# One tile of gathered rows in every 27 quads comes by single-row DMAs of SyncE in place of a GpSimd gather

## The chip, the core and the metric

The kernel runs on one core of a Trainium2 chip. The metric is the device time of one execution in microseconds (us); lower is better. The engines of the core work through instruction lists of their own and meet only at semaphores: TensorE (PE in the profile, PEld for its weight loads), VectorE (DVE), ScalarE (ACT), GpSimd (POOL) and SyncE (SP), which here does nothing but register work and DMA issues. A name with a q behind it (SPq, ACTq) is the instruction queue of an engine.

## What is computed

A graph layer over 12,500 nodes with 160 features each (64 scalars and 32 vectors of three components) and 400,000 edges, sorted by their target node. All is float32.

```python
h_s, h_v = s @ lin1_ws * a, v @ lin1_wv * a            # per node, scaled
w = silu(edge_scalars @ fc_w1) @ fc_w2                 # per edge: 224 weights
es, ev = h_s[edge_src], h_v[edge_src]                  # per edge: one row of the table h
m_s1 = w1 * es * e0;  m_s2 = w4 * einsum(ev, e1)
m_v1 = (w2 * es) * e1;  m_v2 = w3 * ev * e0;  m_v3 = w5 * cross(ev, e1)
agg = segment_sum([m_s1, m_s2, m_v1, m_v2, m_v3], edge_dst)
out = layernorm(x + gated(sc + agg @ lin2))            # per node
```

What matters here is `h[edge_src]`: for each edge a row of 160 floats (640 bytes) of the table `h_table` in DRAM, at an arbitrary place.

## The kernel before, in words

`setup_block` (the first 100 us) scales the weights, computes `h_table` and stores it in DRAM, and loads the edge indices into SBUF. `edge_block` then does all the rest. Its edges, padded, make 3128 tiles of 128 edges, one edge to a partition. Four tiles (`QT`) make a **quad**, 782 in all; eight quads (`RING`) make a **round**, of which there are 97 and a rest of six quads. For a quad q the engines do this, each in its own list:

- GpSimd: `gather` (line 637), one indirect DMA for each tile, which reads 128 rows of `h_table` by the 128 indices of that tile into `rows`, a ring of 8 quads of 4 tiles. Each adds to the semaphore `rows_loaded[q % 8]`. At every second quad the first gather also waits on `tiles_summed`, so that GpSimd is at most about three quads ahead of the sums. Its list is written out in full, all 3128 gathers.
- ScalarE: loads `es` (the edge scalars, once for two quads), the activation `hid`, the copy `tsum` of the tiles' sums, and `copy_out`, which copies the sum of a quad into `aggsb[q % 2]` and signals `agg_copied`. Before it overwrites `aggsb[b]` it waits for the store of two quads earlier (`agg_stored[b]`).
- TensorE, in this order in the list of a quad: `weights` of the next quad (`psw`), for even q `hidden` (`psx`), now and then a piece of node work, `combine` of the quad before (`psg`, lines 955 and 957), and `sum_tiles` of this quad (`pst_e`, line 947), which waits on `prod_ready`.
- VectorE: `products` multiplies the weights in `psw` with the gathered `rows` into `prod` (lines 523, 533, 534) and signals `prod_ready`. It waits on `w_ready` and on `rows_loaded`. Then come the `shifts` (line 804).
- SyncE, one **turn** for each quad (`quad`, lines 549 to 557): read the quad's base row from SBUF into a register (`value_load`, line 549), wait for `agg_copied`, wait until the store before has landed, and store the sum with one DMA of 4 x 32 pieces of 640 bytes whose address is in a register (line 557). In turn 1 of a round come four more DMAs (`node_load`, lines 565 to 568) that load what 128 finished nodes need, in turn 7 one (`node_store`, line 573).

Node work (transposes, `lin2`, gates, layer norm) for 128 nodes goes along with each round from the third on. SyncE, TensorE, ScalarE and VectorE run the rounds in loops (`Fori`), GpSimd does not. An `Else` branch for unusual inputs is not run here.

Of the kernel before, what the change touches and what calls it, by code (L numbers as in the profile page):

```python
# [12 lines left out]
ds = bass.ds  # L13
# [42 lines left out]
PICK = [(B3X, 1), (B2A, 1), (B5X, 2), (B5X, 1)]  # L56

CHUNKS = K4 * F // P

C_W = HID ** -0.5 * 16.0 ** -0.5  # L60
C_S = C_W * SO ** -0.5
# [351 lines left out]
def edge_block(nc, io, m):  # L413

    with ExitStack() as ctx:
        def sb(name, shape, dt=F32):
            return ctx.enter_context(nc.sbuf_tensor(name, shape, dt))

        def sem(name):
            return ctx.enter_context(nc.semaphore(name))  # L420
# [2 lines left out]
        hid = sb("hid", [P, 2 * CH])  # L423
        idx = sb("idx", [P, 1], I32)
        rows = sb("rows", [P, RING * QT, F])
        prod = sb("prod", [P, 2, QT, PW])
        hot = sb("hot", [P, 2, 2 * QT, W8])
        sel = sb("sel", [P, 2, QT, K4, W8])
# [37 lines left out]
        w_ready = sem("w_ready")  # L466
        loads_seen = sem("loads_seen")
        rows_loaded = [sem(f"rows_loaded{u}") for u in range(RING)]
        hot_ready = sem("hot_ready")
        prod_ready = sem("prod_ready")  # L470
        shifts_ready = sem("shifts_ready")
# [71 lines left out]
        @block.sync  # L543
        def _(sp):
            miss = sp.value_load(m.misses[0:1, 0:1], min_val=0, max_val=CHECKS * P)

            def quad(q, i, b, free):

                at = sp.value_load(m.base[0:1, ds(q, 1)], min_val=0, max_val=N - 1)
                sp.wait_ge(agg_copied, q + 1)  # L550
                sp.sem_inc(loads_seen, 1)
                if b:
                    sp.wait_ge(agg_stored[0], 16 * (i + 1))
                elif free:
                    sp.wait_ge(agg_stored[1], 16 * i)
                sp.sem_inc(loads_seen, 1)
                sp.dma_start(m.agg[ds(at, W), :].rearrange("n (k c) -> k n c", k=K4),
                             aggsb[:, b, :]).then_inc(agg_stored[b], 16)

            def node_load(k, width, bufs, c, free):  # L560
                if free:
                    sp.wait_ge(n_res, k)
                sp.sem_inc(loads_seen, 1)
                nodes, r = ds(k * P, width), slice(0, width)
                sp.dma_start(bufs[0][r, :], m.agg[nodes, :]).then_inc(n_in[c], 16)
                sp.dma_start(bufs[1][r, :], io["x"][nodes, :]).then_inc(n_in[c], 16)
                sp.dma_start(bufs[2][:, r], io["xT"][0:S, nodes]).then_inc(n_in[c], 16)
                sp.dma_start(bufs[3][:, r], io["xT"][S:F, nodes]).then_inc(n_in[c], 16)

            def node_store(k, width):  # L570
                sp.wait_ge(n_norm, k + 1)
                sp.sem_inc(loads_seen, 1)
                sp.dma_start(io["out"][ds(k * P, width), :], yn[0:width, :]).then_inc(n_out, 16)

            def round_of(R, quads, first, loading, storing):
                for u in range(quads):
                    quad(R * RING + u, R * (RING // 2) + u // 2, u % 2, not first or u >= 2)
                    if loading and u == 1:
                        node_load(R - 2, P, main_bufs, 0, storing)
                    if storing and u == RING - 1:  # L580
                        node_store(R - 3, P)

            with sp.If(miss == 0):
                round_of(0, RING, True, False, False)
                round_of(1, RING, False, False, False)
                round_of(2, RING, False, True, False)
                with sp.Fori(3, ROUNDS) as R:
                    round_of(R, RING, False, True, True)
                round_of(ROUNDS, REST, False, True, True)
                for b in range(2):  # L590
                    sp.wait_ge(agg_stored[b], 16 * (QUADS // 2))
                node_load(NBLK - 2, P, spare_bufs(0), 1, False)
                node_load(NBLK - 1, LASTN, spare_bufs(1), 2, False)
                for k in range(ROUNDS - 3, NBLK):
                    node_store(k, P if k < NBLK - 1 else LASTN)
                sp.wait_ge(n_out, 16 * NBLK)
            with sp.Else():
                sp.wait_ge(g_zero, 1)
                with sp.Fori(0, AGG_ROWS // P) as b:
                    sp.dma_start(m.agg[ds(b * P, P), :], gsum[:]).then_inc(g_cleared, 16)  # L600
                sp.wait_ge(g_cleared, 16 * (AGG_ROWS // P))

                def tile(q, u, first):
                    if not first:
                        sp.wait_ge(g_added, 16 * (QT * q + u))
                        sp.sem_inc(loads_seen, 1)
                    h = S * (u % 2)
                    sp.dma_start(es[0:S, 0:P], io["esP"][h:h + S, ds(q * CH + P * (u // 2), P)]).then_inc(g_es, 16)
                    sp.dma_start(dstrow[:], io["dst"][ds(QT * q + u, 1), :].to_broadcast([P, P])).then_inc(g_dst, 16)

                for u in range(QT):
                    tile(0, u, u == 0)
                with sp.Fori(1, QUADS) as q:
                    for u in range(QT):
                        tile(q, u, False)
                sp.wait_ge(g_added, 16 * TILES)
                node_load(0, P, main_bufs, 0, False)
                with sp.Fori(1, NBLK - 1) as k:
                    node_store(k - 1, P)
                    node_load(k, P, main_bufs, 0, True)  # L620
                node_store(NBLK - 2, P)
                node_load(NBLK - 1, LASTN, main_bufs, 0, True)
                node_store(NBLK - 1, LASTN)
                sp.wait_ge(n_out, 16 * NBLK)
# [3 lines left out]
        def _(pool):  # L628
# [12 lines left out]
            with pool.If(miss == 0):  # L641
                for q in range(QUADS):
                    for j in range(QT):
                        gather(q, j, max(0, q - 2) if j == 0 and q % GROUP == 0 and q >= GROUP else 0)
            with pool.Else():
                with pool.Fori(0, TILES) as t:
# [128 lines left out]
        def _(dve):  # L775
# [9 lines left out]
            def products(I, u, first):  # L785
# [10 lines left out]
                    sel[:, b, :, :, :], hot[:, u // 2 % 2, QT * b:QT * b + QT, :].unsqueeze(2).to_broadcast([P, QT, K4, W8]),  # L796
                    m.e4[:, ds(q * QT, QT), :].unsqueeze(3).to_broadcast([P, QT, K4, W8]), ALU.mult)
                dve.wait_ge(w_ready, q + 1)
                dve.wait_ge(rows_loaded[u], 16 * QT * (I + 1))
                vec = rows[:, QT * u:QT * u + QT, :]  # L800
                all_products(prod[:, b, :, :], psw[b], vec, QT).then_inc(prod_ready, 1)
                if not first:
# [66 lines left out]
            with dve.If(miss == 0):  # L869
                nc.vector.memset(prod[:, :, :, V * 7:V * 8], 0.0)  # L870
                round_of(0, RING, True, False, False)
                with dve.Fori(1, 3) as I:
                    round_of(I, RING, False, False, False)
                round_of(3, RING, False, True, False)
                with dve.Fori(4, E4_ROUNDS) as I:
                    round_of(I, RING, False, True, True)
                dve.wait_ge(e4_loaded, 16 * E4_PIECES)
                with dve.Fori(E4_ROUNDS, ROUNDS) as I:
                    round_of(I, RING, False, True, True)
                round_of(ROUNDS, REST, False, True, True)  # L880
                node_normalise(ROUNDS - 3, P, True)
# [236 lines left out]
```

## Time and profile before

| | us |
|---|---|
| median of 3 runs | 4938.19 |
| lowest and highest run | 4926.22, 4938.32 |
| span of the profiled execution, first to last instruction | 4099.4 |
| TensorE busy in it | 4024.1 (98%) |
| GpSimd busy in it | 2993.0 (73%) |
| VectorE busy in it | 2439.2 (60%) |
| ScalarE busy in it | 2021.4 (49%) |

The profiled execution has no time of its own on record; beside its span of 4099.4 us stands the median of the runs, 838.8 us longer. This part lies before the first and behind the last instruction, and no row shows it. The granted TensorE clock is 0.995 of full speed over the span. Busy time of TensorE is modelled: consecutive matmuls overlap in the record, so that 98% does not mean that it never waited. SyncE's register work and DMA issues are not counted as busy, and its idle time stands only in the view of who waits for whom.

### The profile page before, as it was taken

The page shows a single profiled execution, that of the slowest core. Times are in us where ns is not written, and L with a number is a line of the kernel's source. Part 1 is how long each engine was busy: PE and PEld are TensorE (multiplying, and loading weights), DVE is VectorE, ACT ScalarE, POOL GpSimd, SP SyncE. Part 2 cuts the span into 40 slices and gives each one's busy share as a digit, 9 for nine tenths or more (in the row PEclk, how much of TensorE's full clock was granted, in tenths as well). Part 3 has the DMA queues.
Part 4 walks back from the last instruction along what each step waited for, and adds up shares of the span by engine and source line. Part 5 has one row for each costly group of instructions (what it writes and reads, how often), then busy time and mean ns, then how long its engine had stood idle before and what let it go on. Part 6 is the DMA issues. An engine that isn't in the chain of part 4 may idle for free.

```text
span 4099.4 us, 69550 instructions
## 1 busy us (share of the span) xinstructions
PE 4024.1 (98%) x15455; PEld 1725.2 (42%) x15455; DVE 2439.2 (60%) x7618; ACT 2021.4 (49%) x5183; POOL 2993.0 (73%) x3139
## 2 busy tenths in 40 slices
PE   8899999999999999999999999999999999999997
PEld 6344444444444444444444444444444444444443
DVE  4556665666666665566566565666666666666564
ACT  3345455555545454545555444545454554545454
POOL 0777777777777777777777777777777777777774
PEclk9999999999999999999999999999999999999998
DMA  7444444444444444444444444444444444444443
GB/s 216 155 123 118 123 119 125 119 123 123 119 124 120 124 119 123 118 123 119 125 119 124 122 119 124 120 123 120 122 119 123 119 125 119 123 124 119 126 118 82
DMA packets 395154, 507.25 MB, mean 124 GB/s; under 512 B 71315, under 2 KB 277904, under 8 KB 394724
## 3 DMA queue, kind: packets, MB, share of 16 engines
q0 software_dynamic: 150144, 256.45, 25.5%
q1 hardware_dynamic: 172386, 133.82, 10.9%
q10 hardware_dynamic: 72578, 116.54, 9.5%
q14 instruction: 38, 0.31, 0.0%
q8 instruction: 8, 0.13, 0.0%
HBM read 426.47 MB, written 80.06 MB: 124 GB/s over the span
## 4 chain that ended last, share of the span: by engine, by line
POOL 69%; issue 22%; PE 4%; DMA 1%; DVE 1%; ACT 0%; ACTq 0%; POOLq 0%; DVEq 0%
POOL rows L637 69%; PE psw L940 1%; PE pst_e L947 1%; DMA rows<-h_table,src_cols 1%; PE psg L955 1%; PE psg L957 1%; PE psx L979 0%; PE psx L931 0%; DMA es<-in_esP 0%; DVE prod L523 0%; ACTq L731 0%; DVE prod L533 0%; DVE prod L534 0%; ACT L701 0%; PE psx L964 0%
## 5 line engine op out<-in xcount | busy, mean ns | idle before, releaser
L637 POOL DMA_INDIRECT rows<-h_table,src_cols x3128 | 2991.4, 956 | 1060.7 <-issue 1050.0
L523 DVE TENSOR_TENSOR prod<-psw,rows 128x384 f32<-128x384 f32 (+2 forms) x3128 | 1212.0, 449 | 1487.3 <-DMA rows<-h_table,src_cols 1413.0
L940 PE MATMUL psw<-fc,hid 128*128 128x480 f32 x3128 | 1471.8, 593 | 1.6 <-ACT hid L671 1.6
L681 ACT ACTIVATE aggsb<-psg 32x160 f32<-32x160 f32 x3128 | 921.7, 295 | 791.6 <-PE psg L957 761.2
L940 PEld LDWEIGHTS psw<-fc,hid 128*128 128x128 f32 x3128 | 531.2, 189 | 909.7 <-issue 836.2
L947 PE MATMUL pst_e<-prod,sel 128*32 128x448 f32 x6256 | 750.7, 552 | 31.6 <-DVE prod L534 29.2
L955 PE MATMUL psg<-tsum,shifts 128*128 128x448 f32 x1564 | 719.2, 541 | 0.7 <-ACT tsum L686 0.7
L957 PE MATMUL psg<-tsum,shifts 128*128 128x448 f32 x1562 | 715.3, 540 | 0.0
L671 ACT ACTIVATE hid<-psx 128x512 f32<-128x512 f32 x391 | 233.6, 597 | 538.2 <-PE psx L931 537.1
L686 ACT ACTIVATE tsum<-pst_e 128x448 f32<-128x448 f32 x782 | 425.6, 544 | 32.2 <-PE pst_e L947 13.3
L957 PEld LDWEIGHTS psg<-tsum,shifts 128*128 128x128 f32 x1562 | 297.0, 190 | 290.4 <-issue 290.4
L931 PE MATMUL psx<-es,fc 128*128 128x512 f32 x782 | 401.4, 595 | 14.4 <-DMA es<-in_esP 14.4
L955 PEld LDWEIGHTS psg<-tsum,shifts 128*128 128x128 f32 x1564 | 274.9, 190 | 257.7 <-issue 256.0
L947 PEld LDWEIGHTS pst_e<-prod,sel 128*32 128x32 f32 x6256 | 123.1, 108 | 549.6 <-DVE prod L534 282.9
L804 DVE TENSOR_TENSOR shifts<-shift,tile_offset 128x256 f32<-128x256 f32 x782 | 323.9, 414 | 0.1
L533 DVE TENSOR_TENSOR prod<-psw,rows 128x256 f32<-128x256 f32 x782 | 322.0, 412 | 0.0
L534 DVE TENSOR_TENSOR prod<-psw,rows 128x256 f32<-128x256 f32 x782 | 321.5, 411 | 0.0
L795 DVE TENSOR_TENSOR sel<-hot,e_cols 128x128 f32<-128x128 f32 x782 | 224.9, 288 | 53.0
L931 PEld LDWEIGHTS psx<-es,fc 128*128 128x128 f32 x782 | 148.8, 191 | 180.9 <-issue 165.3
L671 ACT ACT_TABLE_LOAD x96 | 123.2, 1283 | 185.6 <-PE psx L931 176.7
L979 PEld LDWEIGHTS psx<-w,turned 128*128 128x128 f32 (+1 forms) x980 | 168.2, 194 | 44.4 <-issue 40.4
L979 PE MATMUL psx<-w,turned 128*128 128x192 f32 (+1 forms) x980 | 180.3, 332 | 2.1 <-ACT turned L695 2.1
(112 smaller groups left out, 1158.7 us busy)
## 6 DMA issues: line engine op xcount, KB each, us to landing
es<-in_esP ACTq DMA_DIRECT2D x391, 256.0 KB
agg_table<-aggsb SPq DMA_DIRECT2D x782, 80.0 KB
rows<-h_table,src_cols POOLq DMA_INDIRECT x3128
nag<-agg_table SPq DMA_DIRECT2D x96, 320.0 KB
out<-yn SPq DMA_DIRECT2D x97, 80.0 KB
h_table<-hrow ACTq DMA_DIRECT2D x24, 320.0 KB, 3.2
nxr<-in_x SPq DMA_DIRECT2D x96, 80.0 KB
xa<-in_xT SPq DMA_DIRECT2D x24, 256.0 KB, 2.6
```

The costliest lines, as they stand in the source:

```text
L523: return nc.vector.tensor_tensor(out, w_part, ev, ALU.mult)
L637: nc.gpsimd.indirect_dma_start(out=rows[:, u * QT + j, :], out_offset=None, in_=m.h, in_offset=bass.IndirectOffsetOnAxis(ap=m.src[:, t:t + ...
L671: nc.scalar.activation(hid[:], psx[:], ACT.Silu, scale=HID ** -0.5).then_inc(hid_ready, 1)
L681: ins = nc.scalar.activation(aggsb[r, b, :], picked(psg[r, :], k), ACT.Copy)
L686: nc.scalar.activation(tsum[:, b, :], pst[b][:, 0:PW], ACT.Copy).then_inc(tsum_copied, 1)
L804: nc.vector.tensor_tensor(shifts[:, b, :, :, :].rearrange("p h k n -> p h (k n)"), m.shift[:].rearrange("p k n -> p (k n)").unsqueeze(1).t ...
L931: nc.tensor.matmul(psx[:], m.fc1[:], es[:], start=True, stop=True).then_inc(hid_summed, 1)
L940: ins = nc.tensor.matmul(both[:, 0:256 + WN], hid[:, at:at + P], m.fc2[:], start=True, stop=True)
L947: ins = nc.tensor.matmul(pst[b][W * j:W * j + W, 0:PW], sel[:, b, j, :, :], prod[:, b, j, :], start=True, stop=True, tile_position=(0, W * j))
L955: ins = nc.tensor.matmul(psg[:, 0:PW], shifts[:, b, 0, :, :], tsum[:, b, :], start=True, stop=not before)
L957: ins = nc.tensor.matmul(psg[:, 0:PW], shifts[:, b, 1, :, :], tsum[:, 1 - b, :], start=False, stop=True)
L979: ins = nc.tensor.matmul(out, left, right, start=(n == 0), stop=(n == len(steps) - 1), skip_group_check=True)
```

## The change

It takes 27 of the 3128 gathers off GpSimd's list: the last tile (j = 3) of the quads 47, 74, 101, ... 749. SyncE brings these rows instead. From its turn 16 on it works in periods of 27 turns: in each of the first 26 turns of a period it issues five DMAs of one row each (the last time three), 128 in all, from `h_table` to one partition of the buffer `fetched`, and in the 27th one DMA from `fetched` into the tile's place in `rows`, which is five quads ahead of its use. The indices come by a DMA of 512 bytes into `picks` (a period ahead) and from there into 16 registers at a time, 8 loads in a period. The base rows of the sums are read in the same way, eight registers once in a round in place of one in each turn. VectorE waits for `fetch_placed` before the products of such a quad. The loops of SyncE and VectorE are written out in full. A new input `src` holds the same indices as `srcT` in rows. TensorE's and ScalarE's lists stay as they are.

```diff
+ROWS_A_TURN = 5
+LOADED = 16
+FETCH_TURNS = -(-P // ROWS_A_TURN)
+FETCH_EVERY = FETCH_TURNS + 1
+FETCH_FIRST = 2 * RING
+FETCH_AHEAD = 5
+FETCHED = {q: n for n, q in enumerate(range(FETCH_FIRST + FETCH_TURNS + FETCH_AHEAD, QUADS - RING, FETCH_EVERY))}
+FETCH_TILE = QT - 1
+def gathers_before(q):
+    return sum(QT - (p in FETCHED) for p in range(q % RING, q + 1, RING))
@@ edge_block
+        picks = sb("picks", [1, 2, P], I32)
+        fetched = sb("fetched", [P, 2, F])
@@ SyncE
+            bases = [sp.alloc_register(f"base{i}") for i in range(RING)]
             def quad(q, i, b, free):
-                at = sp.value_load(m.base[0:1, ds(q, 1)], min_val=0, max_val=N - 1)
+                if q % RING == 0:
+                    count = min(RING, QUADS - q)
+                    sp.load(bases[0:count], m.base[0:1, q:q + count])
+                at = sp.snap(bases[q % RING], min_val=0, max_val=N - 1)
                 sp.wait_ge(agg_copied, q + 1)
...
+            pick = [sp.alloc_register(f"pick{i}") for i in range(LOADED)]
+            def fetch_turn(turn):
+                n, part = divmod(turn - FETCH_FIRST, FETCH_EVERY)
+                if turn < FETCH_FIRST or n >= len(FETCHED):
+                    return
+                b = n % 2
+                quad_of = FETCH_FIRST + FETCH_TURNS + FETCH_AHEAD + n * FETCH_EVERY
+                if part == 0:
+                    if n >= 2:
+                        sp.wait_ge(fetch_placed, 16 * (n - 1))
+                    t = quad_of * QT + FETCH_TILE
+                    if n == 0:
+                        sp.dma_start(picks[:, b, :], io["src"][t:t + 1, :]).then_inc(picks_loaded[b], 16)
+                    if n + 1 < len(FETCHED):
+                        t += FETCH_EVERY * QT
+                        sp.dma_start(picks[:, 1 - b, :], io["src"][t:t + 1, :]).then_inc(picks_loaded[1 - b], 16)
+                    sp.wait_ge(picks_loaded[b], 16 * (n // 2 + 1))
+                if part < FETCH_TURNS:
+                    for p in range(part * ROWS_A_TURN, min(P, (part + 1) * ROWS_A_TURN)):
+                        if p % LOADED == 0:
+                            sp.load(pick, picks[:, b, p:p + LOADED])
+                        at = sp.snap(pick[p % LOADED], min_val=0, max_val=N - 1)
+                        sp.dma_start(fetched[p:p + 1, b, :], m.h[ds(at, 1), :]).then_inc(rows_fetched[b], 16)
+                else:
+                    u = quad_of % RING
+                    sp.wait_ge(rows_fetched[b], 16 * P * (n // 2 + 1))
+                    sp.wait_ge(prod_ready, quad_of - RING + 1)
+                    sp.dma_start(rows[:, u * QT + FETCH_TILE, :], fetched[:, b, :]).then_inc(fetch_placed, 16)
...
                     quad(R * RING + u, R * (RING // 2) + u // 2, u % 2, not first or u >= 2)
+                    fetch_turn(R * RING + u)
...
-                with sp.Fori(3, ROUNDS) as R:
+                for R in range(3, ROUNDS):
@@ GpSimd
                     for j in range(QT):
+                        if q in FETCHED and j == FETCH_TILE:
+                            continue
@@ VectorE
-                dve.wait_ge(rows_loaded[u], 16 * QT * (I + 1))
+                dve.wait_ge(rows_loaded[u], 16 * gathers_before(q))
+                if q in FETCHED:
+                    dve.wait_ge(fetch_placed, 16 * (FETCHED[q] + 1))
...
-                with dve.Fori(4, E4_ROUNDS) as I:
+                for I in range(4, E4_ROUNDS):
...
-                with dve.Fori(E4_ROUNDS, ROUNDS) as I:
+                for I in range(E4_ROUNDS, ROUNDS):
```

On SyncE, two turns in a row of the round that is written in the loop before (ISA is register work, TENSOR_LOAD a load of registers from SBUF, and the names in brackets are the semaphores that are waited for):

```order
L549 ISA
L549 TENSOR_LOAD window_base
L549 ISA x2
L550 REGISTER_ALU
L553 ISA [waits agg_copied]
L557 ISA [waits agg_stored0]
L557 DMA agg_table<-aggsb 4x32x160
L549 ISA
L549 TENSOR_LOAD window_base
L549 ISA x2
L550 REGISTER_ALU
L557 ISA [waits agg_copied,agg_stored1]
```

The same engine after the change, one turn of a fetching period (line 582 is the store of the sum, 609 the fetch of a row):

```order
L582 ISA [waits agg_copied,agg_stored0]
L582 DMA agg_table<-aggsb 4x32x160
L608 ISA
L609 DMA fetched<-h_table 1x160
L608 ISA
L609 DMA fetched<-h_table 1x160
L608 ISA
L609 DMA fetched<-h_table 1x160
L608 ISA
L609 DMA fetched<-h_table 1x160
L608 ISA
L609 DMA fetched<-h_table 1x160
```

A turn loses its register load, and five issues, each with one register step ahead of it, stand between one store of a sum and the wait for the next.

On VectorE, after the change, the products of the first fetched quad (47):

```order
L865 TENSOR_TENSOR shifts<-shift,tile_offset 128x256 [waits quad_summed]
L854 TENSOR_TENSOR sel<-hot,e_cols 128x128 [waits tiles_summed]
L543 TENSOR_TENSOR prod<-psw,rows 128x4x3x32 [waits fetch_placed,rows_loaded7,w_ready]
L543 TENSOR_TENSOR prod<-psw,rows 128x4x2x32
L543 TENSOR_TENSOR prod<-psw,rows 128x4x32
```

Only the wait on `fetch_placed` is new there; its rows are moved by nothing else.

## Rows read from the trace of the kernel before

**Rows 1.** The page's chain that ended last: shares of the span by engine, then by line
```profile
POOL 69%; issue 22%; PE 4%; DMA 1%; DVE 1%; ACT 0%; ACTq 0%; POOLq 0%; DVEq 0%
```
**Rows 2.** Who waited for whom, whole span: total us, times, longest us
```profile
DVE prod L523 <- DMA rows<-h_table,src_cols: 1413.0, 751, 9.9
POOL rows L637 <- issue: 1050.0, 3118, 99.9
...
PE pst_e L947 <- DVE prod L534: 29.2, 66, 3.0
...
POOL rows L637 <- PE pst_e L947: 10.7, 10, 7.9
```
**Rows 3.** Line 637, the gathers: ns min/median/max, first and last start in us
```profile
L637 POOL DMA_INDIRECT rows<-h_table,src_cols x3128: 942/949/1200, 102.1 to 4053.4; - x196
```
**Rows 4.** Timeline of PE over one round: start us, us, instruction group [idle before <-releaser]
```profile
2002.47 1.88 PE L940 MATMUL psw<-fc,hid 128*128 128x480 f32 x4
...
2011.25 0.96 PE L947 MATMUL pst_e<-prod,sel 128*32 128x448 f32 x8 [0.23 <-DVE prod L534]
...
2042.79 1.88 PE L940 MATMUL psw<-fc,hid 128*128 128x480 f32 x4
```
**Rows 5.** What SP's own queue waited for, whole span
```profile
SPq L551 <- ACT aggsb L681: 1941.9, 680, 28.3
```
**Rows 6.** SP's instructions of lines 557 and 549: ns min/median/max, first and last start
```profile
L557 SPq DMA_DIRECT2D agg_table<-aggsb x782: 589/612/747, 130.9 to 4066.6; - x196
...
L549 SPq FUSED_REGOPS  x1440: 37/161/175, 101.6 to 4060.6; - x180
L549 SPq TENSOR_LOAD <-window_base x782: 286/675/882, 101.3 to 4059.8; - x196
L549 SPq SEQ_ASSERT  x782: 18/18/23, 101.8 to 4060.8; - x196
```
**Rows 7.** Timeline of SP, turns 7 to 2 of two rounds
```profile
2019.23 0.39 SPq L573 DMA_DIRECT2D out<-yn  x1
2024.75 5.56 SPq L557 DMA_DIRECT2D agg_table<-aggsb  x2
2030.66 0.35 SPq L565 DMA_DIRECT2D nag<-agg_table  x1
2031.22 0.33 SPq L566 DMA_DIRECT2D nxr<-in_x  x1
2031.73 0.58 SPq L567 DMA_DIRECT2D nxs<-in_xT  x1
2032.51 0.43 SPq L568 DMA_DIRECT2D nxv<-in_xT  x1
2034.16 24.96 SPq L557 DMA_DIRECT2D agg_table<-aggsb  x6
```
**Rows 8.** SP's small issues in the setup, by line: ns min/median/max
```profile
L195 SPq DMA_DIRECT2D l1v<-in_lin_wv x4: 413/422/566, 1.4 to 2.9; - x4
...
L199 SPq DMA_DIRECT2D arow<-in_node_vec x1: 551/551/551, 3.7 to 3.7; - x1
L198 SPq DMA_DIRECT2D arow<-in_node_vec x1: 323/323/323, 3.4 to 3.4; - x1
```
**Rows 9.** The page's DMA queues: packets, MB, share of 16 engines
```profile
q0 software_dynamic: 150144, 256.45, 25.5%
q1 hardware_dynamic: 172386, 133.82, 10.9%
q10 hardware_dynamic: 72578, 116.54, 9.5%
q14 instruction: 38, 0.31, 0.0%
```

More of the change, by code:

```diff
@@ L468, in edge_block @@
         rows_loaded = [sem(f"rows_loaded{u}") for u in range(RING)]
+        picks_loaded = [sem(f"picks_loaded{b}") for b in range(2)]
+        rows_fetched = [sem(f"rows_fetched{b}") for b in range(2)]
+        fetch_placed = sem("fetch_placed")
         hot_ready = sem("hot_ready")
@@ L871, in _ @@
                 round_of(0, RING, True, False, False)
-                with dve.Fori(1, 3) as I:
+                for I in range(1, 3):
                     round_of(I, RING, False, False, False)
                 round_of(3, RING, False, True, False)
-                with dve.Fori(4, E4_ROUNDS) as I:
+                for I in range(4, E4_ROUNDS):
                     round_of(I, RING, False, True, True)
                 dve.wait_ge(e4_loaded, 16 * E4_PIECES)
-                with dve.Fori(E4_ROUNDS, ROUNDS) as I:
+                for I in range(E4_ROUNDS, ROUNDS):
                     round_of(I, RING, False, True, True)
@@ L1100 @@
         "x": x, "xT": xT, "xzT": xz.reshape(V, chunks, CB, P).transpose(2, 0, 1, 3).reshape(CB * V, chunks * P),
-        "srcT": src.reshape(TILES, P).T, "dstT": dst.reshape(TILES, P).T, "dst": dst.reshape(TILES, P),
+        "srcT": src.reshape(TILES, P).T, "dstT": dst.reshape(TILES, P).T, "dst": dst.reshape(TILES, P), "src": src.reshape(TILES, P),
         "tile_base": dst.reshape(TILES, P)[:, 0:1].T,
```

## The prediction

> **What bounds the kernel now.** I read first the chain that ended last: 69% of the span is the gathers of GpSimd and 22% the step from one to the next, TensorE has 4% [rows 1]. The view of waits agrees: VectorE waited 751 times, 1413 us in all, for gathered rows, and GpSimd itself waited for another engine only 10 times, 10.7 us in all, of which 7.9 once [rows 2]. From the first gather's start at 102.1 to the last at 4053.4 there are 3127 steps [rows 3]: (3951.3 - 10.7) / 3127 = 1.260 us for a gather, 5.04 for a quad, 40.33 for a round of 32. So a gather left out is worth 1.26 us, if nothing else is next.
>
> TensorE is next, and very near. One round of its list, from one `psw` group at 2002.47 to the one eight quads later at 2042.79, took 40.32 us, and in it TensorE waited once, 0.23 us for VectorE's products, which with the covered start of the group is some 0.3 [rows 4]. Its own work in a round is then 40.0 us. Slack: 0.33 us a round, 32 us over 97.75 rounds. The waits view gives a like figure, 29.2 us in 66 waits [rows 2].
>
> SyncE matters because the change gives it the work. It waited 1941.9 us for the copied sums [rows 5], so of 3936 us between its first and last store [rows 6] it was at work for 1994: 2.55 us of each 5.04 us turn, 20.4 us a round.
>
> **The change, part by part.** *GpSimd* loses 27 gathers: 27 x 1.26 = 34.0 us. Their descriptors go too, and nothing is added to its list.
>
> *TensorE* takes back some of it. In a period of 27 quads its slack is 27/8 x 0.33 = 1.1 us and the gather saved is 1.26, so the two engines come out level, and TensorE's limit of 32 us (29.2 by the waits view) is the lower one. I take 30 us. Gathers may run three quads ahead, so that the unevenness inside a round is covered.
>
> *SyncE, what goes and stays.* A turn in which it didn't wait: from the end of the `nxv` issue (2032.51 + 0.43) to the next store's start at 2034.16 are 1.22 us, and 0.61 for the store itself [rows 6, 7]: 1.83. Of the 1.22 the register load and its steps are 0.675 + 0.161 + 0.037 + 0.018 = 0.89 [rows 6], which go: a turn becomes 0.94, eight 7.5. `node_load` stays at 2.3 (2030.66 to 2032.94), the store of nodes at some 0.6 [rows 7]. Added are, in a round, one load of eight registers and 8 x 8/27 = 2.37 loads of sixteen. No row shows a load of more than one register. Bounds: as long as one (0.675), or as many times as long as it has registers (10.8 for sixteen). I take the one, since it is one instruction and the only row there is: 3.37 x 0.68 = 2.3. The two small DMAs and the copy of a period are 2 x 0.6 x 8/27 = 0.4. Sum without the fetches: 13.1 us a round.
>
> *SyncE, the fetches.* 128 issues in 27 turns are 37.9 a round. Between issues with an address in a register lie 0.18 to 0.21 us (0.56 - 0.35 from `nag` to `nxr`) [rows 7]; I take 0.20. For the issue itself: the cheapest row is 0.32 to 0.33 (97 or 128 rows), the dearest of a regular kind the store of the sum, 0.61 [rows 6 to 8]. The nearest in kind is the one issue of a single row in the setup, 0.551, whose address is fixed [rows 8]. It was the first of its kind; of the four equal issues ahead of it one took 0.566 and the others 0.413 to 0.422 [rows 8]. The fetches come five equal ones in a row, so I take one at 0.55 and four at 0.42, mean 0.44, with the gap 0.64: 24.4 us a round. Bounds: 37.9 x 0.53 = 20.1 and 37.9 x 0.81 = 30.7; with 0.55 for all, 28.4.
>
> *SyncE, sum.* 24.4 + 13.1 = 37.5 us a round against the 40.0 that TensorE needs (bounds without the load question: 33.2 and 43.8). It fits, by 2.5 us. What this hides behind is SyncE's wait for `agg_copied`. In turn 1 of a round it has 0.94 + 3.2 + 2.3 = 6.4 us to do and is late by 1.4, made good in the turns behind. What is queued behind the fetches is the store of the next sum, and ScalarE needs that one only two quads later, about 10 us, so a delay of one or two us reaches nobody. If that cover is gone, each us over the round is a us of the kernel's, since ScalarE's copy, TensorE's `combine` and all else then go at the turns' pace.
>
> *The copy into the ring and the new waits.* The copy is issued in the turn five quads ahead of its use; VectorE is then some three quads, 15 us, from it, and the rows it copies were issued a turn or more earlier. Cost 0. SyncE's wait for the first indices is 2 to 3 us once, inside its slack.
>
> *DMA engines.* 5 packets of 640 bytes in 5 us beside queues that are busy 25.5%, 10.9% and 9.5% of the time [rows 9]: nothing. *The written-out lists:* VectorE and SyncE run some 9,000 and 12,000 instructions without loops. GpSimd's list has that form already and its step stays at the median [rows 3]; the queue of instruction fetches moved 0.31 MB in 38 packets [rows 9]. Cost 0. Of the 838.8 us outside the span no row tells; I leave it as it is.
>
> **The sum.** 4099.4 - 30 = 4069 us of span, and 4938.2 - 30 = 4908 us, a ratio of 0.994. With GpSimd's full 34.0 it would be 4904, with a third of it lost to uneven rounds 4918.
>
> **Rivals.**
> 1. *The single-row issue is as dear alone as in a row* (0.55 or more). SyncE is then the bound: 28.4 + 13.1 = 41.5 us a round, 1.2 over the present 40.33. The periods cover 27 x 27 turns, 91 rounds: +107 us, 5045. At 0.61: 43.8, +316, 5254. It decides from (40.3 - 13.1) / 37.9 = 0.72 us for issue and gap, an issue of 0.52. For it speaks the only single-row row; against it, the four equal ones and the 97-row issue, 0.323, right ahead of it. Chance 0.19.
> 2. *A load of sixteen registers goes register by register.* The row of one register ranges from 0.286 to 0.882 [rows 6], so a good part of it is the way to SBUF, which could be gone for each. If each further register costs 0.1 us, the loads add 2.37 x 1.5 + 0.7 = 4.3 us a round, the round is 41.8 and the kernel 91 x 1.5 = 135 us slower, 5073; by the bound above of 10.8 us a load it would be over 7000. It decides from about 1.9 us for a load of sixteen. Chance 0.18, small for the upper half.
> The Trainium skill ("Runtime: NRT & Kernel Launch", Instruction fetch mechanics) has a rule that speaks against the change here: a TENSOR_LOAD from HBM takes about 200 ns for each register, also in bulk. Ours reads SBUF, and no row shows two registers. By that figure a load of sixteen is 3.7 us (an estimate), the round 46.0 and the kernel near 5450.
> 3. *The gain goes elsewhere*: each gather becomes slower by some ns under the added DMAs. Gathers range from 942 to 1200 ns [rows 3]; 10 ns on each of 3101 is 31 us, the whole gain. Or TensorE's slack is smaller than one round shows. Time 4925 to 4945. Chance 0.16.
> 4. *It doesn't do what it says.* All 27 gathers are gone from the list, so only a late copy could undo it: VectorE would wait in 27 quads. If each waited 5 us, +100 us, 5040. There are 15 us of room. Chance 0.02.
>
> **How the numbers follow.** The forecast (4895 to 4923) has 0.45, rivals 1, 2, 3 and 4 have 0.19, 0.18, 0.16, 0.02. A measurement of this kernel can tell about 0.3% (15 us) from no change. Faster by over 0.3%: 0.45. Within: 0.17, rival 3 and the mildest of 1. Slower: 0.38. The likeliest case's own range is 4895 to 4923. The range has to take in rival 1 whole and the lower half of 2: 4893 to 5280, which leaves out 0.1 to 0.15 above and little below.
>
> **What would show it.** In the new profile: the step between gathers still 1.25 us and GpSimd waiting more for TensorE (tens of us where it was 10.7); TensorE's waits for VectorE near zero. SyncE's wait for `agg_copied` down from 1942 us to some 200 to 300 over the span, not to nothing. The fetch issue's median at 0.42 and the load of sixteen registers under 1.9 us. If SyncE's wait for `agg_copied` is all but gone and ScalarE shows waits for the stored sum, the fetches are too dear and rival 1 or 2 holds, and the two durations tell which. A longer mean gather would show rival 3, a wait of VectorE on the copied tile rival 4. I am wrong if the issue with its gap comes out above 0.72, or the load above 1.9.

## The result, and the profile after

| | before | after |
|---|---|---|
| median of the runs | 4934.48 us (4 runs) | 5655.09 us (4 runs) |
| lowest and highest | 4926.22, 4938.32 | 5629.52, 5671.19 |
| ratio, 95% interval | | 1.1455 (1.1429 to 1.148) |
| span of the profiled execution | see below | 5665.3 us (its time: 5667.55) |

The kernel became 14.6% slower, where 0.6% faster was forecast. The chain that ended last, in the page of the kernel after, shows by engine and by line who has it now:

```profile
SPq 48%; issue 36%; PE 6%; another core or an unknown queue 3%; ACT 3%; DMA 2%; ACTq 0%; DVE 0%; DVEq 0%
SPq L609 21%; SPq L582 8%; SPq L608 7%; SPq L607 3%; PE psg L1016 2%; ACT aggsb L740 2%; DMA nxv<-in_xT 2%; PE psg L1018 2%; SPq L576 1%; SPq L574 1%; SPq L581 1%; PE pst_e L1008 1%; SPq L573 1%; PE psx L1025 1%
```

In [rows 1] GpSimd had 69%; now SyncE has 48%, with the fetches (lines 608, 609) first. The view of waits, SyncE's own and then three rows of the other engines:

```profile
SPq L576 <- ACT aggsb L740: 191.3, 74, 28.8
...
POOL rows L694 <- PE pst_e L1008: 1452.6, 261, 15.1
...
ACT aggsb L740 <- DMA agg_table<-aggsb: 687.7, 172, 9.4
```

SyncE's wait for the copied sums is gone but for 191 us (1941.9 in [rows 5]). ScalarE now waits 688 us for stored sums, a row that the trace before did not have, and GpSimd waits 1453 us for TensorE (10.7 in [rows 2]). So after the change SyncE paces all. But it is not the usual price of a fetch that does it. SyncE's instructions by line, min/median/max in ns:

```profile
L609 SPq MOVE fetched<-h_table x3456: 1/29/1414, 229.1 to 5421.1; - x192
L609 SPq DMA_DIRECT2D fetched<-h_table x3456: 2/225/1422, 229.2 to 5421.1; - x192
...
L607 SPq TENSOR_LOAD <-picks x216: 3/1227/1668, 227.8 to 5396.4; - x108
...
L608 SPq FUSED_REGOPS  x3456: 2/44/1425, 229.0 to 5421.0; - x192
```

The median issue is 0.225 us, half of the 0.44 forecast. The maxima are what is new: a register step with a median of 44 ns takes up to 1425. A DMA issue goes down to 2 ns; I read this as a record that was held up and then came with the next. The timeline of SyncE (start, us, line) shows the five fetches of four turns, two ordinary and two late:

```profile
2999.98 1.95 SPq L609 DMA_DIRECT2D fetched<-h_table  x5
3005.21 0.22 SPq L582 DMA_DIRECT2D agg_table<-aggsb  x1
3006.64 5.19 SPq L609 DMA_DIRECT2D fetched<-h_table  x5
3012.77 0.56 SPq L582 DMA_DIRECT2D agg_table<-aggsb  x1
3013.53 5.95 SPq L609 DMA_DIRECT2D fetched<-h_table  x5
3023.09 0.01 SPq L582 DMA_DIRECT2D agg_table<-aggsb  x1
3023.19 2.27 SPq L609 DMA_DIRECT2D fetched<-h_table  x5
```

Five issues take 1.95 us, or 5.19 and 5.95. In the late turns the trace has single steps 0.7 us apart (at 3007.38, 3008.12, then 3010.26 and 3010.99).

**Which kernel before?** The same source has two times, by the chip it ran on, and all its runs on one chip agree within 0.3%. Each chip was drawn once. On three chips (numbers 12, 4 and 6) it took 4926 to 4936 us, on a fourth (number 2) 4883, and on all of them its span is its time less 2 us; on two others (11 and 8) it took 4094. The trace that stands ahead of the prediction, span 4099.4, is of the second kind; the times beside it, and the result, are of the first. The 838.8 us that the text ahead of the prediction puts before the first and behind the last instruction were this difference; only some 2 us lie there. Below, **slow-stepping** and **even** chips stand for the two kinds, and each run is compared with the kernel before on its own chip only.

### The profile page after: what moved, and what is told of

It is laid out like the page before. It is cut to its first block, busy times and chain, and to the rows that moved or that the text cites. A ratio compares the mean times of both kernels' runs of the same rounds, so it can differ in the third digit from the quotient of the medians.

```text
span 5665.3 us, 71919 instructions
## 1 busy us (share of the span) xinstructions
PE 4513.8 (80%) x15455; PEld 1780.6 (31%) x15455; DVE 2487.4 (44%) x7618; ACT 1996.3 (35%) x5183; POOL 2943.6 (52%) x3112
## 4 chain that ended last, share of the span: by engine, by line
SPq 48%; issue 36%; PE 6%; another core or an unknown queue 3%; ACT 3%; DMA 2%; ACTq 0%; DVE 0%; DVEq 0%
SPq L609 21%; SPq L582 8%; SPq L608 7%; SPq L607 3%; PE psg L1016 2%; ACT aggsb L740 2%; DMA nxv<-in_xT 2%; PE psg L1018 2%; SPq L576 1%; SPq L574 1%; SPq L581 1%; PE pst_e L1008 1%; SPq L573 1%; PE psx L1025 1%
## 5 line engine op out<-in xcount | busy, mean ns | idle before, releaser
L694 POOL DMA_INDIRECT rows<-h_table,src_cols x3101 | 2942.1, 949 | 2676.6 <-PE pst_e L1008 1452.6
L1016 PE MATMUL psg<-tsum,shifts 128*128 128x448 f32 x1564 | 872.3, 643 | 504.4 <-issue 256.2
L1018 PE MATMUL psg<-tsum,shifts 128*128 128x448 f32 x1562 | 831.6, 618 | 0.0
L1008 PE MATMUL pst_e<-prod,sel 128*32 128x448 f32 x6256 | 823.7, 601 | 0.0
L1016 PEld LDWEIGHTS psg<-tsum,shifts 128*128 128x128 f32 x1564 | 272.6, 210 | 899.9 <-issue 458.2
L1025 PE MATMUL psx<-ident,nag 128*128 128x128 f32 x384 | 97.8, 403 | 529.8 <-DMA nxv<-in_xT 528.0
L992 PE MATMUL psx<-es,fc 128*128 128x512 f32 x782 | 416.0, 614 | 88.1 <-ACT turned L754 49.2
L1018 PEld LDWEIGHTS psg<-tsum,shifts 128*128 128x128 f32 x1562 | 339.7, 217 | 352.8 <-issue 352.8
L750 ACT ACTIVATE turned<-psx 128x512 f32<-128x512 f32 x98 | 58.3, 595 | 632.0 <-PE psx L1025 591.2
L1025 PEld LDWEIGHTS psx<-ident,nag 128*128 128x128 f32 x384 | 63.1, 201 | 602.6 <-DMA nxv<-in_xT 596.9
L992 PEld LDWEIGHTS psx<-es,fc 128*128 128x128 f32 x782 | 135.7, 190 | 304.8 <-issue 295.7
```

The lines of the kernel that those rows point to most:

```text
L694: nc.gpsimd.indirect_dma_start(out=rows[:, u * QT + j, :], out_offset=None, in_=m.h, in_offset=bass.IndirectOffsetOnAxis(ap=m.src[:, t:t + ...
L992: nc.tensor.matmul(psx[:], m.fc1[:], es[:], start=True, stop=True).then_inc(hid_summed, 1)
L1008: ins = nc.tensor.matmul(pst[b][W * j:W * j + W, 0:PW], sel[:, b, j, :, :], prod[:, b, j, :], start=True, stop=True, tile_position=(0, W * j))
L1016: ins = nc.tensor.matmul(psg[:, 0:PW], shifts[:, b, 0, :, :], tsum[:, b, :], start=True, stop=not before)
L1018: ins = nc.tensor.matmul(psg[:, 0:PW], shifts[:, b, 1, :, :], tsum[:, 1 - b, :], start=False, stop=True)
```

## The experiments

### The kernel before again, and the written-out lists

`e0_before` is the kernel before, unchanged.

> The kernel before, unchanged, for its own span and granted clock beside its time, since the span of 4099.4 us and the median of 4934 us are 835 us apart, while the kernel after has 5665.3 and 5667.6. If the 835 us lie outside the first and last instruction, the span is 4099 again. If the timed executions run in another regime than the traced one (a lower granted TensorE clock, or slow instructions on SyncE as the trace after shows), the span is 4930 or so and the trace shows where.

Measured on a slow-stepping chip: span 4936.5 us, time 4938.34. One line of SyncE, and its wait for the copied sums:

```profile
L549 SPq FUSED_REGOPS  x1440: 2/158/1657, 101.7 to 4902.3; - x180
...
SPq L551 <- ACT aggsb L681: 575.4, 351, 28.4
```

The late steps are here already (a maximum of 1657 ns where [rows 6] has 175), and SyncE's wait for the copied sums is 575 us, not 1942. The room that the prediction wanted to hide the fetches in did not exist on this chip. The chain:

```profile
another core or an unknown queue 37%; ACT 22%; PE 20%; issue 14%; ACTq 2%; SPq 2%; DMA 1%; DVE 0%; DVEq 0%
```

No GpSimd in it, 69% in [rows 1], but hardly any SyncE either. SyncE's late steps are thus not what paces this kernel. The "unknown queue" is told by the view of waits and by the timeline:

```profile
DVE prod L523 <- remote: 773.1, 193, 6.4
ACT aggsb L681 <- remote: 640.1, 140, 7.8
...
POOL rows L637 <- remote: 563.6, 235, 2.8
```

```profile
3000.90 0.27 PE L970 MATMUL psx<-ident,nag 128*128 128x128 f32 x1
...
3006.10 0.28 ACT L695 ACTIVATE turned<-psx 128x128 f32<-128x128 f32 x1 [4.37 <-remote]
```

`remote` stands where a semaphore rose more than 1.5 us after the last instruction that raises it had ended, so that the view names nobody. Matched with their semaphores, these waits, 3682 us over all engines, are every one for TensorE. In the two lines of the timeline TensorE's transposition ends at 3001.17 and is all that ScalarE waits for, but its semaphore rises at 3006.08. Of the 2595 recorded signals of TensorE in this trace 1475 came over 1 us late, counted from the recorded end of the instruction (ends of matmuls are modelled, so it may be the matmul that was late and not its signal). The trace of [rows 1] has 2 of 3011, and no `remote` row at all.

Then the lists without a fetch, SyncE's and VectorE's together (which includes the eight base rows a round), and each alone:

```diff
-FETCHED = {q: n for n, q in enumerate(range(FETCH_FIRST + FETCH_TURNS + FETCH_AHEAD, QUADS - RING, FETCH_EVERY))}
+FETCHED = {}
```

> The change without a single fetch: GpSimd gathers all 3128 tiles, SyncE reads its base rows eight at a time, the lists of SyncE and VectorE are written out. Theory A (the written-out lists cost, SyncE's instructions come late in bursts of 0.7 us, also in its turns 0 to 15 that fetch nothing): slow register steps on SyncE here too, and the time well over that of before, by 200 us or more if SyncE's slack does not cover them. Theory B (the single-row DMAs cost): the time of before within 15 us.

> As the run of both lists without fetches, but VectorE's rounds are loops again; SyncE's list alone is written out. Theory A1 (SyncE's own list without loops runs late): same slow steps as with both lists. Theory A2 (the two long lists compete for what brings instructions): the slow steps are gone or halved. Theory B: the time of before.

> The kernel before with VectorE's rounds written out and nothing else. Theory A1: the time of before within 15 us and SyncE's steps as fast as before. Theory A2: SyncE, in loops, is not slow either, but VectorE may be; over 50 us slower only if VectorE's instructions come late. Theory B: the time of before.

Measured, same chip: 0.989 of before (0.9861 to 0.9919), 0.9907 (0.9874 to 0.994) and 0.9975 (0.9964 to 0.9986). Theory A falls: SyncE's written-out list, with its fewer instructions in a turn, gains on such a chip, and no long list costs. So all of the loss, 5655 against 4882, is in the fetches and what hangs on them. SyncE's wait and the chain with both lists:

```profile
SPq L576 <- ACT aggsb L740: 2150.6, 489, 27.6
...
another core or an unknown queue 39%; ACT 23%; PE 22%; issue 11%; ACTq 3%; DMA 0%; DVE 0%; SPq 0%; DVEq 0%
```

SyncE's wait grew from 575 to 2151 us and the kernel gained only 54. So the slowness of the kernel before on such a chip (4936 against 4094 us) is not for want of room on SyncE; the chain puts it on the late signals of TensorE.

### Fetches for nothing, steps for nothing, a quarter of the gathers

```diff
...
-                        if q in FETCHED and j == FETCH_TILE:
-                            continue
...
-                if q in FETCHED:
-                    dve.wait_ge(fetch_placed, 16 * (FETCHED[q] + 1))
...
-                    sp.wait_ge(prod_ready, quad_of - RING + 1)
-                    sp.dma_start(rows[:, u * QT + FETCH_TILE, :], fetched[:, b, :]).then_inc(fetch_placed, 16)
...
```

> The change with all its fetches, but GpSimd gathers all 3128 tiles as before; the fetched rows go nowhere (no copy into the ring, no wait on it). Theory S (SyncE is the bound by the steps it gets): within 1% of the change's 5655 us, since the 27 gathers and the copies count for nothing. Theory W (the new waits, on the copied tile or on landed rows, cost): back near the 4882 us of the written-out lists.

For the steps, the body of `fetch_turn` on top of `FETCHED = {}`:

```diff
+                for p in range(part * ROWS_A_TURN, min(P, (part + 1) * ROWS_A_TURN)):
+                    for _ in range(3):
+                        sp.sem_inc(loads_seen, 1)
```

> The written-out lists, all gathers on GpSimd, and for each of the 3456 fetches three semaphore steps of SyncE (the fetch has three instructions: register step, move, DMA), five times in a turn; no register loads, no DMA. Theory S-count (each instruction of SyncE comes late while GpSimd gathers, whatever it is): 5300 to 5600 us. Theory S-DMA (the DMA issues themselves are dear, the rest isn't): under 5000 us.

```diff
-                    for j in range(QT):
+                    for j in range(1):
                         gather(q, j, max(0, q - 2) if j == 0 and q % GROUP == 0 and q >= GROUP else 0)
...
-                dve.wait_ge(rows_loaded[u], 16 * QT * (I + 1))
+                dve.wait_ge(rows_loaded[u], 16 * (I + 1))
...
+                for u in range(RING):
+                    nc.vector.memset(rows[:, u * QT + 1:u * QT + QT, :], 0.0)
```

> The kernel before with only the first of the four gathers of each quad (leaves out three quarters of the gathered rows, which are zero here). Theory G (SyncE's slow steps come from GpSimd's gathers): SyncE's long register steps, 1407 over 200 ns in the trace of before, fall to a third or less, its wait for the copied sums comes back to 1500 us or more, and the span goes to TensorE's own work, near 4060 us, as in the trace before the change. Theory H (the slow steps come from something else, SyncE's own list or the other DMAs): still above 1000 long steps and above 4700 us.

The chip drawn was an even one, before at 4093.98. Measured: 1.0032 (1.002 to 1.0044), 1.0021 (1.001 to 1.0031) and 0.9915 (0.9895 to 0.9935, 4058.63 us). These three expectations were written for a slow-stepping chip and tell nothing of it, but they show that on an even chip all 3456 fetches and the written-out lists cost 13 us when nothing is saved for them, and that the kernel takes 4058 us when TensorE hardly waits for gathered rows. All three were run again on a slow-stepping chip.

> The kernel before with only the first of the four gathers of each quad (leaves out three quarters of the gathered rows, which are zero here). On the second kind of chip 4058 us again. On the first kind: theory G (GpSimd's gathers make SyncE slow) has SyncE's 1407 long steps fall to a third or less and the time to 4060 to 4250 us; theory H (the chip makes SyncE slow whatever GpSimd does) has over 1000 long steps and 4700 us or more.

This time the chip was slow-stepping, before at 4936.24. Measured: 4058.17 us, 0.822 of before (0.8204 to 0.8237), the same time as on the even chip. SyncE's register steps and its wait:

```profile
L549 SPq FUSED_REGOPS  x1440: 37/161/175, 101.9 to 4021.7; - x180
...
SPq L551 <- ACT aggsb L681: 1934.5, 688, 24.9
```

Its steps at line 549 are those of [rows 6] to the ns, and its wait is 1934 us. Theory G holds: with three of four gathers gone the chip's slowness is gone too, TensorE's late signals with it (2 of 2914 over 1 us). It is GpSimd's gathers that hold SyncE and TensorE's signals up there; the run takes away the gathers and their row traffic together and doesn't tell the two apart.

> The written-out lists, all gathers on GpSimd, and for each of the 3456 fetches three semaphore steps of SyncE in place of its three instructions, no DMA and no register load. Where the kernel before takes 4936 us: theory S-count (each instruction of SyncE comes late in a long run of gathers, whatever it is) 5200 to 5600 us; theory S-DMA (the issues are what comes late) 4880 to 5000. Where it takes 4094 us: 4103 again.

Slow-stepping chip, before at 4926.01. Measured: 5303.38 us, 1.0763 (1.0709 to 1.0817). Semaphore steps without a DMA are late as well; from the 0.989 of the lists they add 8.7 points, where the fetches with all gathers kept (the next run) add 14.1. So the count of instructions is over half of it. The fetches have register loads and issues besides, which take longer even on an even chip. Each ratio is against before on its own chip; the three runs were on three chips.

> All fetches, but GpSimd gathers all 3128 tiles too; no copy into the ring and no wait on it. Where the kernel before takes 4930 us: theory S (SyncE's steps are the whole loss) 5600 to 5750; theory W (the new waits are a part of it) under 5500. Where it takes 4094: 4105 again.

Slow-stepping chip, before at 4883.04. Measured: 5519.35 us, 1.1298 (1.1276 to 1.132); SyncE waited 220.8 us for the sums. With all gathers kept, the fetches and the lists are 13.0 of the change's 14.6 points. In us it lies between the two expectations, so neither theory is met to the letter. The other 1.6 points, the copies, the waits or the chip (its time before is 1% off the others), are not told apart.

An earlier `e14_fetch_for_nothing_again` had drawn an even chip:

> All fetches, but GpSimd gathers all 3128 tiles too; no copy into the ring and no wait on it. Where the kernel before takes 4930 us: theory S (SyncE's steps are the whole loss) 5600 to 5750; theory W (the new waits are a part of it) under 5500. Where it takes 4094: 4107 again.

Measured: 1.003 (1.0019 to 1.004).

### What in the gathers does it

I counted, in the records of each trace, SyncE's register, move and semaphore steps after 150 us, and how many of them took over 200 ns, by the place of the gather that GpSimd was at in a row without a pause (0 is the first, - is a time when GpSimd wasn't gathering):

```
kernel, chip               steps  slow |  -    0    1    2    3    4    5    6    7   8 and on
before, even                7962     1 | .02  .00  .00  .00  .00  .00  .00  .00  .00  .00
before, slow-stepping       7966  1393 | .15  .02  .04  .10  .20  .30  .37  .58  .56   -
after, slow-stepping       11026  1560 | .04  .02  .08  .24  .31  .36  .49  .51  .62   -
after, even                11021     1 | .01  .00  .00  .00  .00  .00  .00  .00  .00  .00
a quarter of the gathers    7960    64 | .00  .03  .00   -    -    -    -    -    -    -
```

On the slow-stepping chip GpSimd gathers in rows of eight (389 of them) and then waits for sums; the later in the row, the more of SyncE's steps are late. TensorE's signals go the same way: over 1 us late are next to none beside the first four gathers of a row, and 24, 59, 90 and 98% beside the fifth to the eighth. On an even chip GpSimd gathers 3112 tiles without a pause and nothing is late, so the length of a row does it only on the one kind of chip. Whether shorter rows help:

```diff
-GROUP = 2
+GROUP = 1
```

> The kernel before with GROUP = 1: GpSimd's first gather of every quad, not of every second, waits for the sums three quads back. On a chip with 4936 us GpSimd then gathers in runs of four, not eight. Theory G-run (SyncE is slow from about the fourth gather in a row on: 2% to 8% of its register steps are slow beside the first three, 28% beside the fourth, 40% to 59% beside the fifth to eighth): long steps fall from 1407 to under 900 and the time by 100 to 500 us. Theory G-share (only the share of the time with gathers counts): within 30 us of before. On a chip with 4094 us: the same time within 5 us.

> GROUP = 1 together with the written-out lists and the eight base rows a round, no fetches. Theory G-run on a chip with 4936 us: below the run with GROUP = 1 alone and below 4882, say 4400 to 4750. On a chip with 4094 us: 4090 to 4100.

Slow-stepping chip, before at 4926.01. Measured: 1.0436 (1.0395 to 1.0477) with `GROUP = 1` alone and 1.0003 (0.9983 to 1.0024) with the lists, where the lists alone had 0.989. The slow steps fell from 1393 to 955, not under the 900 of theory G-run, as 236 rows of eight were left beside 307 of four, and the time rose by 205 us, against both theories. GpSimd's waits in the run with `GROUP = 1` alone:

```profile
POOL rows L637 <- issue: 915.4, 2597, 100.0
POOL rows L637 <- PE pst_e L947: 642.4, 293, 8.9
POOL rows L637 <- remote: 543.9, 238, 2.7
```

Its waits for TensorE, `remote` among them, are 1186 us against 957 in `e0_before`, while SyncE waits more for the sums, 1172 us against 575. So the number of SyncE's late steps is not what makes the time of this kernel; my expectation of a gain is refuted. That GpSimd now stands behind one of TensorE's late signals at each quad, not at each second, would explain the loss; no run shows it by itself.

### The change on an even chip

> The kernel after the change, unchanged. Two kinds of chips have shown up: one on which the kernel before takes 4936 us and SyncE's steps come late in bursts of 0.7 us, one on which it takes 4094 us and they don't. Theory C (the change is decided by how fast the chip lets SyncE step): on the first kind again 1.14 to 1.15 of before; on the second 0.990 to 0.998 of before, as the prediction had it (30 us). Theory D (the fetches are dear everywhere): well above before on both.

On a slow-stepping chip: 1.1505 (1.1482 to 1.1527), 0.5 points over the result. The third run:

> The kernel after the change, unchanged, for a chip of the other kind. Where the kernel before takes 4094 us: 4060 to 4075 us (theory C, the forecast's 30 us), or 4100 and more if the fetches cost there what e6_fetch_for_nothing showed (13 us) and TensorE has no slack to give. Where it takes 4930: 5650 to 5690 again.

> The written-out lists with the eight base rows a round and no fetches, for an interval. Where the kernel before takes 4930 us: 4870 to 4895, 0.987 to 0.992 of before. Where it takes 4094: within 5 us of it.

> The change with two rows in a turn in place of five, so that 11 tiles are fetched, one in every 65 quads, and 1408 single-row DMAs in place of 3456. Theory S by the number of steps, where before takes 4930: from the 4882 of the lists with no fetch and the 5655 of the change in proportion, 4882 + 773 x 1408 / 3456 = 5197; if SyncE's slack swallows a small number, 4880 to 4950. Where before takes 4094: 4080 to 4095.

Even chip, before at 4093.56. Measured:

| run | median us | ratio, 95% interval |
|---|---|---|
| the change | 4070.29 | 0.9941 (0.9924 to 0.9957) |
| lists, no fetch | 4098.49 | 1.001 (1.0001 to 1.002) |
| two rows a turn, 11 tiles | 4090.19 | 0.9991 (0.9981 to 1.0002) |

The change goes there the way that was forecast: 23 us less, where 30 were forecast. SyncE's rows in it, its wait, the five fetches of one turn, and who waits for whom:

```profile
L609 SPq DMA_DIRECT2D fetched<-h_table x3456: 217/225/304, 209.7 to 3849.1; - x192
...
L607 SPq TENSOR_LOAD <-picks x216: 1153/1244/1692, 208.3 to 3834.8; - x108
...
L608 SPq FUSED_REGOPS  x3456: 44/44/60, 209.5 to 3849.0; - x192
...
SPq L576 <- ACT aggsb L740: 928.9, 541, 27.6
...
2001.51 1.94 SPq L609 DMA_DIRECT2D fetched<-h_table  x5
```

```profile
DVE prod L543 <- DMA rows<-h_table,src_cols: 1289.5, 672, 9.7
...
POOL rows L694 <- PE pst_e L1008: 18.0, 23, 7.4
...
PE pst_e L1008 <- DVE prod L554: 6.0, 8, 1.8
```

The same instructions, no late ones (the maximum of a register step is 60 ns), and SyncE still waits 929 us. TensorE waits 6 us for VectorE, 29.2 in [rows 2], and the chain is TensorE's:

```profile
PE 82%; POOL 10%; issue 3%; DMA 1%; DVE 0%; SPq 0%; ACT 0%; ACTq 0%; POOLq 0%; DVEq 0%
```

The parts, all on this chip: the lists +4.9 (4098.49); the fetches with all gathers kept +6.8 more (4105.32 in `e14`); and from there to the change -35.0, which is what the 27 gathers left out give less what the copies and waits cost. The prediction had 27 x 1.26 = 34.0 for them.

The two rows were meant for a slow-stepping chip, so how the loss goes with the number of fetches there stays open.

### Base rows in batches, loops kept

```diff
...
-                at = sp.value_load(m.base[0:1, ds(q, 1)], min_val=0, max_val=N - 1)
+                if u == 0:
+                    sp.load(bases[0:quads], m.base[0:1, ds(q, quads)])
+                at = sp.snap(bases[u], min_val=0, max_val=N - 1)
...
```

> The kernel before, loops kept, but SyncE loads its eight base rows once a round in place of one in each turn. Theory S-count: five instructions of each turn become two or so, about as much as in the written-out lists, so 4880 to 4910 us. If the gain of the written-out lists came from the missing loops and register arithmetic: 4925 to 4940.

Even chip: 1.0002 (0.9992 to 1.0011), nothing. SyncE has slack there, and the expectation was for the other kind. Which part of SyncE's new list gains 0.9% on a slow-stepping chip, the missing register loads or the missing loop, is open.

## Why the prediction was wrong, point by point

- **What bounds the kernel: wrong for the chip that was measured.** The step that failed is taking the trace for the execution that is timed: GpSimd as the bound with 69% of the chain, SyncE with 1941.9 us of room, and the 838.8 us of which the prediction says "no row tells; I leave it as it is". A span 17% under the time was no overhead: it said that the trace and the times came from executions that ran differently. On the chips of the result GpSimd waits. In the kernel before, the others wait there for late signals of TensorE (37% of the chain, SyncE 2%); after the change SyncE's steps have the chain (48%).
- **SyncE's room: wrong in the same way.** 1941.9 us of waiting in [rows 5] are 575.4 on a slow-stepping chip. The forecast's "It fits, by 2.5 us", 37.5 us of SyncE's work in a round of 40.0, was worked from steps that are never late. Measured after the change, from the first to the last store (131.3 to 5635.1 us, less the wait of 191.3, over 781 turns), SyncE's work was 54.4 us a round.
- **GpSimd: right on an even chip.** 27 x 1.26 = 34.0 us were forecast, and 35.0 lie between the fetches for nothing and the change.
- **TensorE's limit: nearly right there.** Its room was put at 32 us; before is 35.4 us over the 4058.6 of the quarter of the gathers. 4070 is 12 us over that; its waits for VectorE fell from 29.2 to 6.0 us, and the chain went over to it.
- **The issue of one row: too dear.** Forecast 0.44 with bounds from 0.32; measured 0.225, below the lower bound. With its gap it is (1.94 - 0.22) / 4 = 0.43 from the timeline of the even chip, not 0.64. A single row has the lowest median of all SyncE's issues, and why the one in [rows 8] took 0.551 no run tells.
- **The load of sixteen registers: too cheap.** Forecast 0.675, measured 1.244, a mean of 38 ns for each further register; a load of eight (line 573) took 0.772, so the step is not even. That is under the 1.9 us at which rival 2 decides. The Trainium skill ("Runtime: NRT & Kernel Launch", Instruction fetch mechanics) has about 200 ns for each register of a load from HBM. These loads read SBUF, and that figure does not carry over to them.
- **SyncE's sum on an even chip.** 37.9 x 0.43 + 13.1 + 2.37 x 0.57 = 30.7 us a round, a wait of 9.3; measured 929 us over 98 rounds, 9.5. The two errors, one term too high and one too low, left the sum of 37.5 about 7 us too high.
- **The sum on an even chip.** Ratio 0.994 forecast, 0.9941 measured. That they are the same is luck: the forecast's 30 us were divided by 4938, the measured 23 by 4094. The written-out lists (4.9 us) and the fetches (6.8) were costed at nothing, and the gathers gave 35 and not the 30 to which TensorE was to hold them.
- **Rivals.** SyncE as the bound, at the place named and with the signs named (its wait gone, ScalarE waiting for the stored sum), is what happened on a slow-stepping chip, but by neither of the two prices: both durations that were to tell which came out on the cheap side. What was missing was a rival in which a step of SyncE depends on what GpSimd does, and one in which the trace is of another kind of execution than the times. The price, 5655 us, was beyond the range.

## What to carry to other kernels

Where the profiled span and the timed median are far apart, find out why before anything is costed: the rows then describe another execution than the one that is timed. An engine that only issues DMAs can be paced by another engine's work, so its idle time in one trace is no promise of room, and work moved to it should be as few instructions as can be. Nor does room on one engine make a kernel faster: with the written-out lists SyncE waited 1575 us longer and the time fell by 54. Where a view names nobody for a wait, find out whose semaphore it is before a pace is put down to the engine that looks odd. A rewrite that cuts the issuing engine's instructions (here the lists without fetches: 0.989 on a slow-stepping chip, 1.001 on an even one) is the safer half of such a change, while the fetches themselves are only worth having on an even chip (0.994).

## What the runs showed of the hardware

- On some of the chips SyncE's instructions come 0.7 us apart in bursts while GpSimd gathers by indirect DMA, and on others never: 1393 of 7966 steps over 200 ns against 1. The same program takes 20% longer there (4936 and 4094 us).
- It hits SyncE's steps and TensorE's signals, and the others not. In the trace of `e0_before` 1475 of 2595 recorded signals of TensorE came over 1 us after the recorded end of their instruction, 2 of 3011 on an even chip. The signals of ScalarE and VectorE come there with a median of 8 and 11 ns, as on an even chip, no register or semaphore step of ScalarE or GpSimd took over 200 ns, and of VectorE at most 2. Many signals are missing from the traces of slow-stepping chips (2595 recorded of 3031 by TensorE, 1474 of 2445 by ScalarE).
- It grows with the number of gathers in an unbroken row, from 2% of SyncE's steps beside the first to over 50% beside the seventh and eighth (TensorE's signals: from next to none to 98%), and it vanishes with three quarters of the gathers. What GpSimd, SyncE and TensorE share there, and why some chips don't show it, no run tells.
- TensorE's granted clock was 0.995 of full speed in the trace of [rows 1], 0.965 in `e0_before` and 0.913 after the change. Its busy share fell with it (98%, 88%, 80%). 3% less clock does not make 20% more time, so the clock is not the cause of the slow kind; whether the idle stretches lowered it is not shown.
- A single-row issue of SyncE with its address in a register took 0.225 us, 0.43 with the steps before it. Loads of 1, 8 and 16 registers from SBUF took 0.675, 0.772 and 1.244 us (medians on even chips).
